# GpSimd's residual sums without the wait for the unpacking of the last weight block

## The chip, the cores and the metric

One core of a Trainium2 chip. The metric is the device time of the program in microseconds; the median of three runs counts. The profile shows one execution, with a span (first to last instruction) a little shorter than its device time.

## The reference

The input x has 64 batches of 64 rows by 1024 columns. Each batch picks one of 16 condition matrices (64 x 64), which mixes its rows; the result goes through a linear layer with a 1024 x 1024 weight, given as packed 6-bit integers with a scale and a zero point for each output column, and is added to x:

```python
def cond(x, weights, condition):
    W = weights[condition]
    return jnp.einsum('bct,bcd->bdt', x, W)

def ffn(x, qweight, weight_scale, weight_zero_point, bias):
    w = dequantize(qweight)   # four 6-bit values from three int32 words
    w = (w - zero_point) * scale
    return jnp.einsum('bsk,nk->bsn', x, w) + bias

x = x + ffn(cond(x, cond_weights, itok), qweight, scale, zero_point, bias)
```

## The kernel before, in words

Two batches make one tile of 128 rows, so there are 32 tiles (counted from 0). Four tiles are in flight in rings of four buffers (`RING`). The work of a tile goes round the engines:

- SyncE's queue loads x (`x_sb`) and two condition matrices (`w_sb`), and stores the two halves of the output.
- TensorE mixes (`mix`, line 264), which also transposes, into PSUM (`y_ps`). ScalarE copies that to `y_hi` (line 415) and VectorE writes the remainder `y_lo` (`low`, line 507). TensorE then multiplies both with the unpacked weight `qT`, one half of the output columns at a time (`linear`, `products`, line 306), into `o_ps`.
- ScalarE sums the rows of x (`sum_x`), TensorE mixes those sums (`sum_y`), and VectorE uses them for the zero point.
- GpSimd writes x plus the bias to `resid` (`add_bias`, line 624). VectorE adds the zero-point term to `resid` (`residual`, line 516), scales the products from PSUM into `o_sb` (`scale_out`, line 527) and adds `resid` to them (`add_residual`, line 535).

The weight comes in eight blocks of 128 output columns (`NT` is 8, blocks 0 to 7). For each, VectorE unpacks the words into 16-bit integers with three instructions (`unpack_q`, lines 495, 497 and 499, each adding 1 to the semaphore `q_part`), TensorE transposes them (`transpose_q`, line 288), and ScalarE places them in `qT` (`place_q`, line 429). These blocks are woven by hand into the work of the first tiles. VectorE's order there is: blocks 0 to 3, low parts of tile 0, the zero-point rows, blocks 4 to 6, low parts of tile 1, scaling of tile 0's first half, block 7, scaling of tile 1's first half, low parts of tile 2, then residuals. TensorE's order is: the first products of tile 0, mix of tile 1, block 4, rest of tile 0's first half, block 5, `sum_y(0)`, block 6, half of tile 1's products (these reuse the bank that the scaling of tile 0 frees), block 7, the other half, mix of tile 2, and so on. After tile 3 loops take over, with two tiles to a step.

On GpSimd the program clears two buffers, builds the identity, waits for the bias (loaded by SyncE's queue after the weight blocks), waits for all of `q_part`, and then adds the bias to tile after tile. Tiles 0 to 3 wait only for their x; from tile 4 on a sum also waits until VectorE has written the output of the tile four before, whose buffer it takes. A reload of an x buffer waits, among other things, for the sum of the tile before in it (`xbias_ready`). Every engine works through its own list in order.

Of the kernel before, what the change touches and what calls it, by code (L numbers as in the profile page):

```python
# [31 lines left out]
def adaln_ffn(nc: bass.Bass, x, cond, weights, qweight, scale, zero, bias, out):  # L32
    B, C, K = x.shape
    NCOND, _, S = weights.shape
    N, KP = qweight.shape
    assert C == S == P // 2 and N == K
    G = KP // 3
    KT = K // P
    NT = N // P
# [13 lines left out]
    with ExitStack() as ctx:  # L53
# [6 lines left out]
        def sem(name):  # L60
            return ctx.enter_context(nc.semaphore(name))
# [54 lines left out]
        q_part = sem("q_part")  # L116
# [18 lines left out]
        def x_arrived(eng, j, i):  # L135

            eng.wait_ge(x_loaded[j % RING], (i + j // RING + 1) * 16)
# [9 lines left out]
        def _(sp):  # L147
# [31 lines left out]
            def store_last():  # L179
                t = TILES - 1  # L180
                store(t % RING, t // RING, 0)
                for n, (_, col, width) in enumerate(last_pieces):
                    sp.wait_ge(o_ready[1], t + 1 + n)
                    sp.dma_start(out_rows[t * P:(t + 1) * P, col:col + width],
                                 o_sb[:, t % 2, col:col + width]).then_inc(o_stored[1][t % 2], 16)
# [423 lines left out]
        @block.gpsimd  # L609
        def _(pool):  # L610
            nc.gpsimd.memset(w_sb[:], 0.0).then_inc(w_zeroed, 1)
            nc.gpsimd.memset(ident[:], 0.0).then_inc(blank_ready, 1)
            pool.wait_ge(blank_ready, 1)
            nc.gpsimd.affine_select(out=ident[:], in_=ident[:], compare_op=ALU.not_equal, fill=1.0, base=0,
                                    pattern=[[-1, P]], channel_multiplier=1).then_inc(ident_ready, 1)
            pool.wait_ge(bias_loaded, 16)
            pool.wait_ge(q_part, 3 * NT)

            def add_bias(j, i):
                x_arrived(pool, j, i)  # L620
                if not isinstance(i, int) or i * RING + j >= RING:
                    for h in range(H):
                        pool.wait_ge(o_ready[h], i * RING + j - RING + 1)
                nc.gpsimd.tensor_tensor(resid[:, j % RING, :], x_sb[:, j % RING, :], bias_bc[:],  # L624
                                        ALU.add).then_inc(xbias_ready, 1)

            for j in range(RING):
                add_bias(j, 0)
            with pool.Fori(1, TRIPS) as i:
                for j in range(RING):  # L630
                    add_bias(j, i)
# [23 lines left out]
```

## Time and profile before

| what | value |
|---|---|
| median of 3 runs | 298.5 us |
| lowest, highest | 298.39, 301.09 us |
| the profiled execution's own time | 301.04 us |
| its span | 299.1 us |
| TensorE busy | 293.5 us (98%) |
| VectorE busy | 185.2 us (62%) |
| GpSimd busy | 90.7 us (30%) |
| ScalarE busy | 78.9 us (26%) |

The page gives the granted clock of TensorE as full in all of its 40 slices. Busy time is the time in which an engine has at least one instruction in work. Matmuls overlap, so TensorE's 98% means that it hardly ever stood idle, not that it worked at its peak. PE is TensorE, DVE is VectorE, ACT is ScalarE, POOL is GpSimd, and SPq is SyncE's queue.

### The profile page before, as it was taken

To read this page: it belongs to the slowest core of one execution; us is meant where nothing else is said; L and a number is where in the kernel's file an instruction comes from. 1 tells how busy PE (TensorE), PEld (TensorE's weight loads), DVE (VectorE), ACT (ScalarE), POOL (GpSimd) and SP (SyncE) were. 2 spreads that over 40 slices of the span, in tenths; PEclk is the share of its full clock that TensorE was granted. 3 is DMA by queue.
4 is the path that set the end of the run, shared out by engine and by line. 5 is a ranking of instruction groups with operands and counts; after the bars stand their busy time and mean duration, and the time that the engine had idled before them with its cause. 6 is when DMAs were issued, how large, how long until landed. Compare 5 with 4: busy or idle time off the path is not lost.

```text
span 299.1 us, 8384 instructions
## 1 busy us (share of the span) xinstructions
PE 293.5 (98%) x3245; PEld 243.5 (81%) x3245; DVE 185.2 (62%) x254; ACT 78.9 (26%) x171; POOL 90.7 (30%) x39
## 2 busy tenths in 40 slices
PE   8999998999999999999999999999999999999995
PEld 3688876888888888888888888888888888888885
DVE  3544896675656656585665667565665658566554
ACT  3438324250503204050402305050320505020000
POOL 1005844234334042434314143433404243430000
PEclk9999999999999999999999999999999999999999
DMA  6950175452442515234342425234241520111211
GB/s 241 328 223 15 65 249 206 168 181 77 147 147 83 172 70 182 105 113 144 139 134 82 153 105 173 82 142 147 84 170 70 184 105 35 70 72 60 82 70 70
DMA packets 20404, 38.49 MB, mean 129 GB/s; under 512 B 6820, under 2 KB 7076, under 8 KB 20390
## 3 DMA queue, kind: packets, MB, share of 16 engines
q1 hardware_dynamic: 20098, 37.50, 36.4%
q10 hardware_dynamic: 292, 0.79, 0.7%
q8 instruction: 10, 0.16, 0.2%
q14 instruction: 4, 0.03, 0.0%
HBM read 21.50 MB, written 16.78 MB: 128 GB/s over the span
## 4 chain that ended last, share of the span: by engine, by line
PE 93%; DVE 4%; issue 2%; ACT 0%; DVEq 0%
PE o_ps L306 75%; PE y_ps L264 11%; PE y_ps L329 2%; PE ysum_ps L278 2%; DVE resid L516 1%; PE qt_ps L288 1%; PE o_ps L288 1%; DVE y_lo L507 1%; PE ysum_ps L326 1%; PE o_ps L329 1%; PE y_ps L306 1%; DVE o_sb L527 1%; DVE o_sb L535 1%; ACT y_hi L415 0%; DVE o_sb L603 0%
## 5 line engine op out<-in xcount | busy, mean ns | idle before, releaser
L306 PE MATMUL o_ps<-qT,y_hi 128*128 128x512 f32 (+1 forms) x520 | 201.2, 391 | 1.1 <-DVE o_sb L527 1.1
L306 PE MATMUL o_ps<-qT,y_lo 128*128 128x512 f32 (+1 forms) x520 | 199.0, 387 | 0.0
L624 POOL TENSOR_TENSOR resid<-x_sb,bias_bc 128x1024 f32<-128x1024 f32 x32 | 89.5, 2802 | 176.6 <-DVE o_sb L535 152.5
L306 PEld LDWEIGHTS o_ps<-qT,y_hi 128*128 128x128 f32 x520 | 98.0, 190 | 20.9 <-DVE o_sb L527 1.2
L306 PEld LDWEIGHTS o_ps<-qT,y_lo 128*128 128x128 f32 x520 | 98.0, 190 | 18.8
L527 DVE TENSOR_TENSOR o_sb<-o_ps,scale_bc 128x512 f32<-128x512 f32 x63 | 43.6, 692 | 85.0 <-PE o_ps L306 84.9
L415 ACT ACTIVATE y_hi<-y_ps 128x512 fp32r<-128x512 f32 x64 | 33.4, 602 | 175.3 <-PE y_ps L264 175.3
L535 DVE TENSOR_TENSOR o_sb<-o_sb,resid 128x512 f32<-128x512 f32 x63 | 51.7, 820 | 2.3
L507 DVE TENSOR_TENSOR y_lo<-y_ps,y_hi 128x512 fp32r<-128x512 f32 x64 | 40.0, 684 | 13.1 <-ACT y_hi L415 13.1
L516 DVE SCALAR_TENSOR_TENSOR resid<-zs_bc,ysum,resid 128x1024 f32<-128x1024 f32 x32 | 41.9, 1310 | 0.0
L264 PE MATMUL y_ps<-w_sb,x_sb 64*64 64x64 f32 x2048 | 35.1, 223 | 0.0
L406 ACT ACTIVATE junk<-x_sb 128x1024 bf16<-128x1024 f32 x32 | 34.1, 1089 | 0.0
L264 PEld LDWEIGHTS y_ps<-w_sb,x_sb 64*64 64x64 f32 x2048 | 32.5, 138 | 1.7 <-issue 1.5
L278 PEld LDWEIGHTS ysum_ps<-xsum,w_sb 128*128 128x128 f32 x64 | 9.7, 189 | 1.4
L278 PE MATMUL ysum_ps<-xsum,w_sb 128*128 128x1 f32 x64 | 8.5, 230 | 0.0
L495 DVE TENSOR_SCALAR q_int<-q_raw 128x256 int16<-128x256 int16 x8 | 3.6, 455 | 6.6 <-DMA q_raw<-in_L_ffn_qweight_dram 6.6
L406 ACT ACTIVATION_READ_ACCUMULATOR junk<-x_sb 128x1 f32 x32 | 7.4, 231 | 0.0
L424 ACT ACTIVATE ysum<-ysum_ps 128x1 f32<-128x1 f32 x32 | 4.5, 202 | 3.9 <-PE ysum_ps L278 3.9
L429 ACT ACTIVATE qT<-o_ps 128x1024 fp32r<-128x1024 int16 x4 | 4.1, 1028 | 4.0 <-PE o_ps L288 4.0
L288 PEld LDWEIGHTS o_ps<-ident,q_int 128*128 128x128 bf16 x32 | 2.4, 118 | 3.3 <-issue 1.8
L429 ACT ACTIVATE qT<-qt_ps 128x1024 fp32r<-128x1024 int16 x4 | 4.1, 1030 | 0.4 <-PE qt_ps L288 0.4
L497 DVE TENSOR_SCALAR q_int<-q_raw 128x256 int16<-128x256 int16 x8 | 4.0, 501 | 0.0
(32 smaller groups left out, 40.2 us busy)
## 6 DMA issues: line engine op xcount, KB each, us to landing
x_sb<-in_x_dram SPq DMA_DIRECT2D x32, 512.0 KB, 3.5
out_dram<-o_sb SPq DMA_DIRECT2D x63, 256.0 KB, 2.0
q_raw<-in_L_ffn_qweight_dram SPq DMA_DIRECT2D x6, 384.0 KB, 4.9
w_sb<-in_L_cond_weights_dram SPq DMA_DIRECT2D x64, 16.0 KB, 2.0
q_raw<-in_L_ffn_qweight_dram ACTq DMA_DIRECT2D x2, 384.0 KB, 5.4
bias_bc<-in_L_ffn_bias_dram SPq DMA_DIRECT2D x1, 512.0 KB, 7.4
out_dram<-o_sb SPq DMA_DIRECT2D x2, 128.0 KB, 1.9
ids<-in_itok_B_dram SPq DMA_DIRECT2D x1, 0.2 KB
```

What stands on the lines that cost most here:

```text
L264: last = nc.tensor.matmul(y_ps[part * Q:(part + 1) * Q, j % 2, half, kt, :], x_sb[rows, slot, k0:k0 + Q], w_sb[rows, slot, rows], start=Tr ...
L278: nc.tensor.matmul(ysum_ps[:, slot:slot + 1], w_sb[:, slot, :], xsum[:, slot:slot + 1], start=True, stop=True).then_inc(ysum_ps_ready, 1)
L288: last = nc.tensor.transpose(qt_banks[n % 2][:, kt, :], q_cols[:, n % 4, kt * P:(kt + 1) * P], ident[:])
L306: last = nc.tensor.matmul(bank, part[:, slot, kt, :], qT[:, kt, col:col + width], start=(kt == 0 and part is y_hi), stop=(kt == KT - 1 and ...
L329: nc.tensor.matmul(bank, ones[:], row[:, h * NH:(h + 1) * NH], start=True, stop=True).then_inc(row_ps_ready, 1)
L406: nc.scalar.activation(junk[:, j % 2, :], x_sb[:, j % RING, :], ACT.Copy, accum_out=xsum[:, j % RING:j % RING + 1]).then_inc(xsum_ready, 1)
L415: nc.scalar.activation(y_hi[:, j % RING, :, cols], y_ps[:, j % 2, half, :, :], ACT.Copy).then_inc(y_hi_ready, 1)
L507: nc.vector.tensor_tensor(y_lo[:, j % RING, :, cols], y_ps[:, j % 2, half, :, :], y_hi[:, j % RING, :, cols].bitcast(F32), ALU.subtract).t ...
L516: nc.vector.scalar_tensor_tensor(resid[:, j % RING, :], zs_bc[:], ysum[:, j % RING:j % RING + 1], resid[:, j % RING, :], ALU.mult, ALU.add ...
L527: nc.vector.tensor_tensor(o_sb[:, j % 2, cols], o_ps[:, h, :], scale_bc[:, cols], ALU.mult).then_inc(scaled[h], 1)
L535: nc.vector.tensor_tensor(o_sb[:, j % 2, cols], o_sb[:, j % 2, cols], resid[:, j % RING, cols], ALU.add).then_inc(o_ready[h], 1)
L624: nc.gpsimd.tensor_tensor(resid[:, j % RING, :], x_sb[:, j % RING, :], bias_bc[:], ALU.add).then_inc(xbias_ready, 1)
```

## The change

GpSimd no longer waits until all 24 unpacking instructions (three for each of the eight blocks) are done before its first sum. The wait for the bias and each sum's wait for its x stay.

```diff
             pool.wait_ge(bias_loaded, 16)
-            pool.wait_ge(q_part, 3 * NT)
 
             def add_bias(j, i):
                 x_arrived(pool, j, i)
```

## Rows read from the trace of the kernel before

**Rows 1.** The page: span, and busy us by engine.

```profile
span 299.1 us, 8384 instructions
PE 293.5 (98%) x3245; PEld 243.5 (81%) x3245; DVE 185.2 (62%) x254; ACT 78.9 (26%) x171; POOL 90.7 (30%) x39
```

**Rows 2.** Waits, whole span: engine, line, waited for, us, times, longest.

```profile
POOL resid L624 <- DVE q_int L499: 24.1, 1, 24.1
...
PE o_ps L306 <- DVE o_sb L527: 1.1, 1, 1.1
```

**Rows 3.** Timeline of DVE, 31 to 46 us: start, duration, operation.

```profile
31.46 1.29 DVE L507 TENSOR_TENSOR y_lo<-y_ps,y_hi 128x512 fp32r<-128x512 f32 x2 [1.16 <-ACT y_hi L415]
32.66 1.52 DVE L516 SCALAR_TENSOR_TENSOR resid<-zs_bc,ysum,resid 128x1024 f32<-128x1024 f32 x1
34.28 2.70 DVE L535 TENSOR_TENSOR o_sb<-o_sb,resid 128x512 f32<-128x512 f32 x1
36.91 1.27 DVE L516 SCALAR_TENSOR_TENSOR resid<-zs_bc,ysum,resid 128x1024 f32<-128x1024 f32 x1
38.29 0.69 DVE L535 TENSOR_TENSOR o_sb<-o_sb,resid 128x512 f32<-128x512 f32 x1
...
45.44 0.67 DVE L527 TENSOR_TENSOR o_sb<-o_ps,scale_bc 128x512 f32<-128x512 f32 x1
```

**Rows 4.** Timeline of POOL, 26 to 37 us: the first and fourth sum.

```profile
26.00 2.39 POOL L624 TENSOR_TENSOR resid<-x_sb,bias_bc 128x1024 f32<-128x1024 f32 x1 [24.09 <-DVE q_int L499]
...
33.06 3.38 POOL L624 TENSOR_TENSOR resid<-x_sb,bias_bc 128x1024 f32<-128x1024 f32 x1
```

**Rows 5.** The bias: its issue in the timeline, and its landing by tile.

```profile
10.85 0.44 SPq L199 DMA_DIRECT2D bias_bc<-in_L_ffn_bias_dram  x1
...
DMA to landing us min/median/max: 7.4/7.4/7.4
```

**Rows 6.** Timeline of PE, 25 to 46 us.

```profile
25.12 0.48 PE L306 MATMUL o_ps<-qT,y_hi 128*128 128x512 f32 x1
...
27.05 0.62 PE L288 MATMUL o_ps<-ident,q_int 128*128 128x128 bf16 x8
...
43.61 1.16 PE L264 MATMUL y_ps<-w_sb,x_sb 64*64 64x64 f32 x64
...
46.16 0.50 PE L306 MATMUL o_ps<-qT,y_hi 128*128 128x512 f32 x1 [1.08 <-DVE o_sb L527]
```

**Rows 7.** Timeline of DVE, 18 to 26 us: end of block 5, block 6, block 7.

```profile
18.08 0.47 DVE L499 TENSOR_SCALAR q_int<-q_raw 128x512 int16<-128x512 int16 x1
18.47 0.46 DVE L495 TENSOR_SCALAR q_int<-q_raw 128x256 int16<-128x256 int16 x1
18.70 0.51 DVE L497 TENSOR_SCALAR q_int<-q_raw 128x256 int16<-128x256 int16 x1
18.99 0.47 DVE L499 TENSOR_SCALAR q_int<-q_raw 128x512 int16<-128x512 int16 x1
22.39 1.29 DVE L507 TENSOR_TENSOR y_lo<-y_ps,y_hi 128x512 fp32r<-128x512 f32 x2 [2.93 <-ACT y_hi L415]
24.24 0.69 DVE L527 TENSOR_TENSOR o_sb<-o_ps,scale_bc 128x512 f32<-128x512 f32 x1 [0.57 <-PE o_ps L306]
24.85 0.45 DVE L495 TENSOR_SCALAR q_int<-q_raw 128x256 int16<-128x256 int16 x1
...
25.38 0.48 DVE L499 TENSOR_SCALAR q_int<-q_raw 128x512 int16<-128x512 int16 x1
```

**Rows 8.** The chain of work that ended last, by time: start, us, what.

```profile
16.97 3.52 PE o_ps L306 x16
...
22.25 1.96 PE o_ps L306 x16
```

## The prediction

> **What bounds the kernel now.** I read the busy line first: TensorE is busy for 293.5 of 299.1 us, so a change is worth only what it adds to or takes from TensorE's idle time or the length of its work [rows 1]. Then the waits: GpSimd's sums sat behind the unpacking of the last weight block for 24.1 us, the wait that the change removes, and nothing in TensorE's list names GpSimd. TensorE's one large wait behind another engine's work in the steady run is 1.1 us, for VectorE's scaling of an output tile [rows 2]. Last the timelines of the four engines between 18 and 46 us. The reader is to see there that GpSimd and VectorE hold each other up, and which of these waits reach TensorE.
>
> How they hold each other up: VectorE's first residual addition (line 535) took 2.70 us at 34.28, where the same form takes 0.69 us [rows 3]. It therefore began at 34.28 + 2.70 - 0.69 = 36.29 us, while GpSimd's fourth sum ended at 33.06 + 3.38 = 36.44 us [rows 4]. That sum was itself about 1.0 us longer than the 2.39 us of the first: VectorE's line 516, issued at 32.66 and finished at 34.18, had gone ahead of it [rows 3, 4]. So for operations of VectorE with two inputs in SBUF, one of the two waits until the other has quite finished. Line 507, with one input in PSUM, took 1.29 us for two at 31.46, in the middle of the third sum, and wasn't held up [rows 3]: it still costs 0.64 us apiece.
>
> **What the change removes.** The sums may start once the bias has landed: its DMA is issued at 10.85 and lands 7.4 us later, at 18.25 us [rows 5]. Tile 0 and 1 of x were requested before it on the same queue. GpSimd began 0.14 us after what it waited for (25.86 to 26.00), so the four sums move from 26.0 to 36.4 us to about 18.4 to 28 us: 7.6 us earlier [rows 4, 7]. No instruction is added or dropped.
>
> **The gain.** TensorE waits 1.08 us before 46.16 for the scaling of tile 1's second half, which VectorE starts at 45.44 and finishes 0.67 us later [rows 3, 6]. VectorE was busy without a gap worth naming from 31.46 to there, and inside this stretch it lost 1.52 - 1.27 = 0.25 us to the third sum and 2.70 - 0.69 = 2.01 us to the fourth [rows 3]. With the sums over by 29 us, both go: 2.26 us. The scaling could then begin at 43.2, but the products that it reads end only where TensorE's next mix starts, at 43.61 [rows 6]. So it begins at about 43.7 and ends at about 44.4, before TensorE asks for it at 46.16 - 1.08 = 45.08. The whole 1.08 us goes, and no more: what is late next is TensorE's own work. GpSimd's fifth sum, triggered by VectorE's output of tile 0, moves along with VectorE and keeps its place relative to it. The x tiles of the second round are requested earlier, since that request waits for the first sum, and this hides behind work that TensorE has until then; it is worth nothing.
>
> **The cost.** Two unpackings now lie beside the sums: block 6 (18.47 to 19.46) and block 7 (24.85 to 25.86) [rows 7]. Each is three instructions of one input in SBUF, and no row of this trace shows such a one beside a sum; that is the disputed price. Below: nothing, if they don't meet. Above: a whole sum for each meeting, 2.3 us or so. I take it that they meet, because of their pace: starts 0.39 us apart for 512 columns (18.08 to 18.47) and 0.23 for 256 (18.47 to 18.70) make 0.16 / 256 = 0.6 ns a column, against (1270 - 690) / 512 = 1.1 ns for lines 516 and 535 [rows 3, 7]. They move about two elements where the others move one, so something more of the port is used.
>
> The Trainium skill says the same from the other side (VectorE: DVE Perf Modes, Mode 2x_2P; SBUF — State Buffer, Who interferes with whom): a one-source operation from SBUF to SBUF with an even outermost count takes both port pairs, one of which is GpSimd's, and the one that starts first blocks the other fully. By that rule this change puts a lock in front of the unpacking, and it speaks against the change; the pace and the 2.70 us above agree with it, the unpacking beside a sum is not shown.
>
> What is queued behind a held unpacking: VectorE works in order. Behind block 6 stand the low parts of tile 1 (22.39, two of 0.65 us) and the scaling of tile 0 (24.24 to 24.93), whose bank TensorE takes for tile 1 at 25.12: 0.2 us of cover [rows 6, 7]. Behind block 7 stands TensorE itself, which transposes it at 27.05: 1.2 us of cover after 25.86 [rows 6, 7].
>
> Now in turns. At the end of the third sum the waiting line 516 was served ahead of the fourth [rows 3, 4]. I assume the same both ways: whoever waits goes next, also between two unpacking instructions. A sum holds VectorE off for about 2.3 us (2.39 less the 0.15 us between 36.29 and 36.44), an instruction of the unpacking holds off the sum for 0.25 to 0.4 us. GpSimd is ready at 18.4, in the middle of the row of unpackings; three places of entry:
> (a) Before block 6's first instruction: sum 0 to 20.7, first instruction to 20.95, sum 1 to 23.2, second to 23.5, sum 2 to 25.8, third to 26.2; the low parts to 27.5, the scaling to 28.1, block 7 after sum 3 (28.5) to 29.5. TensorE starts tile 1 at 28.2 in place of 25.12: 3.1 us late; block 7 is in time for it.
> (b) After the first: third instruction done at 24.0, low parts 25.2, scaling 25.8; block 7's first at 26.5, sum 3 to 28.8, its last at 29.5. TensorE transposes at 29.55 in place of 27.05: 2.5 us late.
> (c) After the second: block 6 done at 21.7, nothing of it felt; block 7 as in (b): 2.45 us late.
> I take 2.5 us. Less the gain of 1.08, this is +1.4 us (+2.0 for (a)).
>
> **The sum.** The profiled execution took 301.04 us for a span of 299.1; the median of the runs is 298.5 and the highest 301.09, so the profiled one is at the slow edge. I add the difference to the median: 298.5 + 1.4 = 299.9 us. A median of a few runs of this kernel can be told from no change at about 1%, 3 us, so nearly every case here lies within that.
>
> **The rivals.**
> - Unpacking in one piece: VectorE, once served, keeps the port for its three pipelined instructions (their starts are closer than their durations of 0.46 us [rows 7], which speaks for it). Block 7 then starts at 26.3 and is done 1.0 us later at 27.3: 0.2 us late. 0.2 - 1.1 = -0.9: 297.6 us.
> - No meeting at all, so the change doesn't have the cost that I see: -1.1, 297.4 us. Against it stands the pace of the unpacking.
> - GpSimd holds on (slower): its four sums are queued without a wait between them, and if it keeps the port through all four, VectorE is held from 18.4 to about 27.8. Block 6 is done at 28.8, low parts 30.1, scaling 30.8: TensorE takes tile 1 5.7 us late; +4.6, 303.1 us. It makes the kernel slower by over 1% from the point at which TensorE is held there for over 4.1 us. Against it: line 516 got in ahead of the fourth sum [rows 3, 4].
> - TensorE's pace falls: at 16.97 sixteen products of 256 columns took 3.52 us, and the same sixteen at 22.25 took 1.96 us, a ratio of 1.8, near that of 2.4 to 1.2 GHz, while the page shows the granted clock full throughout [rows 8]. If an idle stretch of 2.5 to 3 us near 27 brings back a slow stretch as long as that one, it adds 3.52 - 1.96 = 1.6 us: +3.0, 301.5 us. Against it: the idle 1.08 us before 46.16 changed nothing, though it is shorter.
>
> **How the numbers follow.** Turns 0.44 (299.9, 299.5 to 300.5 by the place of entry), one piece 0.26, no meeting 0.12, GpSimd holds on 0.08, slow pace 0.06, something unseen 0.04. The range reaches from the two gaining cases with a little spread, 297.1, to the slow pace, 301.6, and leaves out GpSimd holding on and the unseen. Faster by over 1% would need 3 us where only 1.1 us of idle time is there: 0.03. Slower by over 1%: GpSimd holding on, half of the slow pace, and a share of the unseen: 0.13. Within 1%: 0.84.
>
> **What the profile of the changed kernel would show.** GpSimd's first sum at 18.3 to 18.5; if later, my landing time is off. Unpacking instructions of block 6 or 7 that last about 2.5 us in place of 0.46, one between every two sums (turns), one at the head of a block alone (one piece), or none (no meeting). TensorE's idle stretch before the transposes at 27.05 or before tile 1's products at 25.12: 2 to 3 us, or 0.2. No wait of TensorE before linear products at 46, and line 535's first at 0.69 us. The pace of products after the idle stretch: starts 0.23 us apart or twice that. The forecast is wrong if GpSimd is not let in between unpackings, or if TensorE's wait at 46 stays, for instance because the fifth sum now meets VectorE in a worse place.

## The result, and the profile after

The changed kernel took 303.05 us (median of 4 runs, 302.66 to 303.94) against 298.44 us before: a ratio of 1.0133 (95% interval 1.0068 to 1.0199). By the two medians it is 4.6 us slower, by the ratio 4.0 us, and the interval lies wholly above 1; forecast was 299.9 us, range 297.1 to 301.6. The two profiled executions are nearer to each other: 301.04 us (span 299.1) before, 303.94 us (span 302.0) after.

The page of the changed kernel, its span and busy line:

```profile
span 302.0 us, 8384 instructions
PE 295.0 (98%) x3245; PEld 244.5 (81%) x3245; DVE 189.7 (63%) x254; ACT 79.0 (26%) x171; POOL 90.1 (30%) x39
```

TensorE's large waits, but for one of 1.2 us in the warm-up that both kernels have:

```profile
PE o_ps L306 <- DVE o_sb L527: 1.3, 1, 1.3
PE qt_ps L288 <- DVE q_int L499: 1.2, 1, 1.2
```

Against [rows 2], the one wait of 1.1 us late in the weaving is gone, and two others have come, both earlier, both behind VectorE: for block 6 of the weight, and for the scaling of tile 0. (The line `o_ps L306 <- DVE o_sb L527` looks as before, but it is another wait, at 27.89.)

VectorE's timeline, the answer to [rows 7] and the first part of [rows 3]:

```profile
18.08 0.47 DVE L499 TENSOR_SCALAR q_int<-q_raw 128x512 int16<-128x512 int16 x1
18.47 2.63 DVE L495 TENSOR_SCALAR q_int<-q_raw 128x256 int16<-128x256 int16 x1
20.90 2.66 DVE L497 TENSOR_SCALAR q_int<-q_raw 128x256 int16<-128x256 int16 x1
23.35 2.59 DVE L499 TENSOR_SCALAR q_int<-q_raw 128x512 int16<-128x512 int16 x1
25.86 1.27 DVE L507 TENSOR_TENSOR y_lo<-y_ps,y_hi 128x512 fp32r<-128x512 f32 x2
27.06 0.68 DVE L527 TENSOR_TENSOR o_sb<-o_ps,scale_bc 128x512 f32<-128x512 f32 x1
27.66 0.83 DVE L495 TENSOR_SCALAR q_int<-q_raw 128x256 int16<-128x256 int16 x1
...
38.14 0.69 DVE L535 TENSOR_TENSOR o_sb<-o_sb,resid 128x512 f32<-128x512 f32 x1
```

The three instructions of block 6 last 2.63, 2.66 and 2.59 us where they lasted 0.46, 0.51 and 0.47. The two low parts at 25.86 and the scaling at 27.06 are not longer at all, though GpSimd is still adding: each has one of its two inputs in PSUM. They are only late. And the first residual addition, 2.70 us before, takes 0.69 us.

GpSimd's four sums in the same time:

```profile
18.23 2.54 POOL L623 TENSOR_TENSOR resid<-x_sb,bias_bc 128x1024 f32<-128x1024 f32 x1 [16.32 <-DMA bias_bc<-in_L_ffn_bias_dram]
20.73 2.50 POOL L623 TENSOR_TENSOR resid<-x_sb,bias_bc 128x1024 f32<-128x1024 f32 x1
23.19 2.47 POOL L623 TENSOR_TENSOR resid<-x_sb,bias_bc 128x1024 f32<-128x1024 f32 x1
25.62 2.54 POOL L623 TENSOR_TENSOR resid<-x_sb,bias_bc 128x1024 f32<-128x1024 f32 x1
```

The first starts with the landing of the bias. Each of the three instructions of block 6 was held through one sum and ended as the next began: 18.47 + 2.63 = 21.10, 20.90 + 2.66 = 23.56, 23.35 + 2.59 = 25.94, each about 0.35 us after the start of the next sum. So it is one instruction of the one engine, then one of the other.

TensorE, to be laid beside [rows 6]:

```profile
26.00 0.62 PE L288 MATMUL qt_ps<-ident,q_int 128*128 128x128 bf16 x8 [1.23 <-DVE q_int L499]
27.89 0.77 PE L306 MATMUL o_ps<-qT,y_hi 128*128 128x512 f32 x1 [1.26 <-DVE o_sb L527]
28.45 0.63 PE L306 MATMUL o_ps<-qT,y_lo 128*128 128x512 f32 x1
28.88 0.63 PE L306 MATMUL o_ps<-qT,y_hi 128*128 128x512 f32 x1
...
31.15 0.62 PE L288 MATMUL o_ps<-ident,q_int 128*128 128x128 bf16 x8
...
49.08 0.48 PE L306 MATMUL o_ps<-qT,y_hi 128*128 128x512 f32 x1
```

The products of tile 1 start at 27.89 in place of 25.12, 2.77 us late. They then start 0.43 us apart (28.45 to 28.88) where the fast pace is 0.23, so that block 7's transposes are at 31.15 in place of 27.05: 4.10 us late. The products at 49.08, before at 46.16, are 2.92 us late: 1.18 us have come back. From there to the end both executions take the same time (302.0 - 49.08 and 299.1 - 46.16, both 252.9 us), so the whole loss lies ahead of it. The windows show the granted clock (the figure ahead of the last two) over this stretch:

```profile
28.00:32.00 4.00, 4.00 (x18) 3.11 (x19) 1.03 (x3) 0.91 (x3) 0.16 (x1) 0.65 0.06 12
32.00:36.00 4.00, 4.00 (x79) 3.42 (x78) 1.13 (x2) 2.08 (x4) 0.00 (x0) 1.00 0.01 4
```

In 28 to 32 us it is 0.65 of full on average, so most of the stretch ran at the level of 1.2 GHz and the rest at 2.4. Just before, TensorE had been idle for 1.23 us (up to 26.00) and for 1.26 us (up to 27.89).

### The profile page after: what moved, and what is told of

Same layout as the page of the kernel before. It is cut to its first block, busy times and chain, and to the rows that moved or that the text cites. A ratio compares the mean times of both kernels' runs of the same rounds, so it can differ in the third digit from the quotient of the medians.

```text
span 302.0 us, 8384 instructions
## 1 busy us (share of the span) xinstructions
PE 295.0 (98%) x3245; PEld 244.5 (81%) x3245; DVE 189.7 (63%) x254; ACT 79.0 (26%) x171; POOL 90.1 (30%) x39
## 4 chain that ended last, share of the span: by engine, by line
PE 95%; DVE 4%; issue 1%; DVEq 0%
PE o_ps L306 77%; PE y_ps L264 11%; PE y_ps L329 2%; PE ysum_ps L278 2%; DVE q_int L495 1%; DVE q_int L497 1%; PE ysum_ps L326 1%; PE o_ps L329 1%; PE qt_ps L288 1%; PE y_ps L306 1%; PE o_ps L288 0%; DVE y_lo L507 0%; DVE q_int L499 0%; DVE o_sb L527 0%; DVE o_sb L603 0%
## 5 line engine op out<-in xcount | busy, mean ns | idle before, releaser
L306 PE MATMUL o_ps<-qT,y_hi 128*128 128x512 f32 (+1 forms) x520 | 202.1, 392 | 1.3 <-DVE o_sb L527 1.3
L306 PE MATMUL o_ps<-qT,y_lo 128*128 128x512 f32 (+1 forms) x520 | 199.7, 388 | 0.0
L306 PEld LDWEIGHTS o_ps<-qT,y_hi 128*128 128x128 f32 x520 | 98.5, 191 | 21.3 <-DVE y_lo L507 1.4
L306 PEld LDWEIGHTS o_ps<-qT,y_lo 128*128 128x128 f32 x520 | 98.6, 191 | 19.0
L527 DVE TENSOR_TENSOR o_sb<-o_ps,scale_bc 128x512 f32<-128x512 f32 x63 | 43.6, 691 | 86.0 <-PE o_ps L306 85.8
L535 DVE TENSOR_TENSOR o_sb<-o_sb,resid 128x512 f32<-128x512 f32 x63 | 49.6, 788 | 2.3
L495 DVE TENSOR_SCALAR q_int<-q_raw 128x256 int16<-128x256 int16 x8 | 6.2, 775 | 6.4 <-DMA q_raw<-in_L_ffn_qweight_dram 6.4
L497 DVE TENSOR_SCALAR q_int<-q_raw 128x256 int16<-128x256 int16 x8 | 6.1, 767 | 0.0
L429 ACT ACTIVATE qT<-o_ps 128x1024 fp32r<-128x1024 int16 x4 | 4.1, 1024 | 7.1 <-PE o_ps L288 7.1
L499 DVE TENSOR_SCALAR q_int<-q_raw 128x512 int16<-128x512 int16 x8 | 5.8, 727 | 0.0
```

The lines of the kernel that those rows point to most:

```text
L306: last = nc.tensor.matmul(bank, part[:, slot, kt, :], qT[:, kt, col:col + width], start=(kt == 0 and part is y_hi), stop=(kt == KT - 1 and ...
L495: nc.vector.tensor_scalar(to[:, :, 0], words[:, :, 0, 0], QMASK, None, ALU.bitwise_and).then_inc(q_part, 1)
L497: nc.vector.tensor_scalar(to[:, :, 1], words[:, :, 0, 0], QBITS, QMASK, ALU.logical_shift_right, ALU.bitwise_and).then_inc(q_part, 1)
L527: nc.vector.tensor_tensor(o_sb[:, j % 2, cols], o_ps[:, h, :], scale_bc[:, cols], ALU.mult).then_inc(scaled[h], 1)
L535: nc.vector.tensor_tensor(o_sb[:, j % 2, cols], o_sb[:, j % 2, cols], resid[:, j % RING, cols], ALU.add).then_inc(o_ready[h], 1)
```

## The experiments

Ratios are against the kernel before, run beside each on the same chip. The kernel before has three groups of times: of 85 executions 23 took 297.2 to 297.6 us, 26 took 298.1 to 298.8, and 36 took 300.75 us or more (all but one under 301.6). A median of a few runs can fall into any of them.

**The kernel before again, and the change again.** No edit.

> The kernel before, unchanged, to learn how far its executions differ. Theory (turns at the port, and TensorE's slower pace after an idle stretch of 2.5 us): a ratio of 1.00, median 298.4 us, and no unpacking instruction over 0.6 us. What is open: the profiled execution of before took 301.0 us against 298.4 of the median. If its early stretch at the slow pace (16.97, 3.52 us for 16 products) is what differs, a faster profiled execution shows that stretch shorter. Rival (the loss of the change is drift between executions): ratio off 1 by as much as the change's 1.013.

Measured: 299.64 us, ratio 1.0014 (0.997 to 1.0058). So the change's 4.0 us and more are not drift. This profiled execution took 297.51 us, span 295.6, and is of the lowest group. The chain of work that ended last (start, us, what):

```profile
15.08 1.97 PE o_ps L306 x16
18.69 1.96 PE o_ps L306 x16
```

The first sixteen products of 256 columns take 1.97 us here, at 15.08, and took 3.52 us at 16.97 in the profile before [rows 8]. The next sixteen take 1.96 us in both, only 3.56 us earlier here, and the executions are 3.53 us apart. So what separates the lowest group from the highest, as far as one profile of each shows, is when TensorE's early slow pace ends, at 20.4 us or before 14.5, before the sums even begin. The middle group of the kernel before has no profile. The Trainium skill says (TensorE: Matmul & The Clock Gate, Part 1, The HAM clock gate) that the watch on its activity runs freely and doesn't start with the kernel; a spread of this kind agrees with that.

> The changed kernel again, in more rounds. Theory: TensorE starts tile 1's products 2.8 us late, has a slow stretch that costs 1.4 us more, and gets 1.1 us back at 46: +3.1 us, ratio 1.010, and up to 1.015 where before happens to run without a slow stretch of its own. Rival (drift between executions): a ratio of 1.00 within 0.003.

Measured: 303.0 us (301.84 to 305.35), ratio 1.0105 (1.0057 to 1.0153). The loss is there again, 3.1 us by the ratio and 4.4 by the medians. The profiled execution, 305.35 us, is the longest of all: block 6 was held as before (2.64, 2.66 and 2.59 us), but the slow stretch lasted longer, with a granted clock of 0.50 in 28 to 32 us and still 0.53 in 32 to 34. No execution of the changed kernel is in the two lower groups: its lowest of all is 301.84 us.

**The change a third time.** No edit.

> The changed kernel once more, for a profile of an execution whose early slow stretch ends early, if it is one. Theory: then block 6 is done before the first sum and isn't held, and block 7 is held at each of its three instructions; a slow stretch follows where TensorE was idle for over 2.5 us. Rival (VectorE is held at the same place in every execution): block 6 is held as in the two profiles so far.

Measured: 303.45 us, span 301.5. It was again an execution with a long early slow stretch, so that it doesn't test what happens after a short one. But here the bias landed later, the first sum started at 18.77 in place of 18.23, and VectorE's timeline shows another place of entry:

```profile
18.47 0.46 DVE L495 TENSOR_SCALAR q_int<-q_raw 128x256 int16<-128x256 int16 x1
...
18.99 2.58 DVE L499 TENSOR_SCALAR q_int<-q_raw 128x512 int16<-128x512 int16 x1
...
24.74 1.75 DVE L495 TENSOR_SCALAR q_int<-q_raw 128x256 int16<-128x256 int16 x1
26.29 2.61 DVE L497 TENSOR_SCALAR q_int<-q_raw 128x256 int16<-128x256 int16 x1
```

Two instructions of block 6 are through before the sum gets in, and only the third is held. The low parts are then in time, and it is block 7 that is late: held by 1.3 and by 2.1 us, and TensorE waits 2.1 us for it. A slow stretch followed here too, from about 30.6, though the idle time was less than the 2.5 us of the expectation. Half a microsecond of the bias decides where VectorE is caught, and TensorE loses its two to three microseconds either way.

**The sums wait for block 6 only.**

```diff
             pool.wait_ge(bias_loaded, 16)
+            pool.wait_ge(q_part, 3 * (NT - 1))
```

> The sums wait for block 6 but not for block 7. Theory of turns: block 6's three instructions are at 0.46 us again, block 7's first instruction waits from 24.85 to about 26.6, the fourth sum goes between the first and the second, the block is done at about 29.5; TensorE transposes it at 29.6 in place of 27.05 (2.5 us late); less 1.1 us at 46: +1.4 us, or +2.9 with a slow stretch after the idle time (299.9 to 301.3). Rival (VectorE keeps the port for its three pipelined instructions): block 7 done at 27.6, +0.5 - 1.1 = -0.6 us (297.8). Rival (the loss came through something else than the port, say the earlier x loads): as slow as the change, 303.

Measured: 303.53 us, ratio 1.0131 (1.0083 to 1.0178): no better than without any wait. VectorE's timeline, and TensorE's wait for block 7:

```profile
22.18 1.34 DVE L495 TENSOR_SCALAR q_int<-q_raw 128x256 int16<-128x256 int16 x1
23.32 2.63 DVE L497 TENSOR_SCALAR q_int<-q_raw 128x256 int16<-128x256 int16 x1
25.75 2.56 DVE L499 TENSOR_SCALAR q_int<-q_raw 128x512 int16<-128x512 int16 x1
```

```profile
PE o_ps L288 <- DVE q_int L499: 3.8, 1, 3.8
```

This execution had another start than both profiles of before: the pace was fast from about 12, the granted clock fell at 15.0, with TensorE at work, and was full again at 18.4. So block 7 came at 22.2 and not at 24.85, under the second sum and not under the third, and was held three times. The mechanism is the one expected, turn by turn, its size 1.3 us larger; a slow stretch followed. The forecast of +1.4 to +2.9 us was too low, and the rival of one piece is out. The other rival, that the loss comes from something else such as the earlier x loads, had forecast 303 us, and the time alone fits it; the 3.8 us that TensorE waits for held unpackings speak against it, and so does the next run.

Block 6 was done at 17.41 here, and the first sum waited for the bias, until 18.45. The added wait had no effect, so this is also what the changed kernel does after such a start. The profiled execution took 302.73 us. The profiles of two_in_gap, halves, only_writes and filled have the same start and no other slow stretch on record, and their granted clock over the whole execution is 0.993 or 0.994; the executions of before at 0.992 to 0.994 are its middle group, 298.1 to 298.8 us. If they start alike, the change costs about 4.3 us there.

**Two sums in the gap.** As above, and the third sum waits for block 7:

```diff
             for j in range(RING):
+                if j == 2:
+                    pool.wait_ge(q_part, 3 * NT)
                 add_bias(j, 0)
```

> The sums of tiles 0 and 1 wait for block 6 only and fall into the gap between blocks 6 and 7 (19.5 to 24.85 us, two sums of 2.4), the sums of tiles 2 and 3 wait for block 7 as before. Theory: no unpacking instruction is held, the first residual addition takes 0.69 us in place of 2.70, TensorE's wait of 1.08 us before 46.16 is gone: -1.1 us, 297.3, ratio 0.996. Rival (early sums cost by themselves, through the x loads that they release): slower than before. If the second sum ends after 24.85, block 7 is late by the difference, which its cover of 1.2 us hides.

Measured: 297.6 us, ratio 0.9967 (0.9927 to 1.0006), so by the interval it is not told from no change. Set side by side by clock it stands out: eight of the twelve executions took 297.0 to 297.9 (most of them 297.0 to 297.4) at a granted clock of 0.992 to 0.994, where those of before at that clock took 298.3 to 298.8. If a like clock means a like early stretch, that is about 1.1 us less, the wait that the prediction counted on. VectorE's timeline:

```profile
22.06 0.99 DVE L495 TENSOR_SCALAR q_int<-q_raw 128x256 int16<-128x256 int16 x1
22.84 0.50 DVE L497 TENSOR_SCALAR q_int<-q_raw 128x256 int16<-128x256 int16 x1
...
31.25 0.69 DVE L535 TENSOR_TENSOR o_sb<-o_sb,resid 128x512 f32<-128x512 f32 x1
```

Block 7's first instruction meets the end of the second sum and is held 0.5 us, which its cover hides, and the first residual addition takes 0.69 us. TensorE has no wait behind VectorE left after the warm-up. Two early sums with their early x loads cost nothing that can be measured here, which speaks against the rival of the early loads (those released by the sums of tiles 2 and 3 stay late in this run).

**Sums cut into pieces.** For tiles 0 to 3, `PIECES` instructions on a share of the columns, with a second semaphore (`xpart`) that keeps the waits of VectorE and SyncE's queue complete. The main part of the edit:

```diff
-                nc.gpsimd.tensor_tensor(resid[:, j % RING, :], x_sb[:, j % RING, :], bias_bc[:],
-                                        ALU.add).then_inc(xbias_ready, 1)
+                pieces = PIECES if first else 1
+                for n in range(pieces):
+                    cols = slice(n * K // pieces, (n + 1) * K // pieces)
+                    nc.gpsimd.tensor_tensor(resid[:, j % RING, cols], x_sb[:, j % RING, cols], bias_bc[:, cols],
+                                            ALU.add).then_inc(xbias_ready if n == pieces - 1 else xpart, 1)
```

> The changed kernel, with the sums of tiles 0 to 3 cut into two instructions of 512 columns each. Theory of turns, instruction by instruction: an unpacking instruction waits for one half sum (about 1.25 us) and not 2.4, so block 6's three last about 1.4 us each and the block is done near 22.4, before the low parts need VectorE; block 7's three are spread over about 3.8 us from 24.85 and TensorE gets it 1.6 us late: +0.6 us against before, or +2 with a slow stretch. Rival (the port time of a tile's sum counts as a whole, however it is cut): block 6 as late as in the change, 25.9, and a ratio of 1.010 to 1.013.

Measured: 301.05 us, ratio 1.0044 (0.9994 to 1.0094). Block 7 on VectorE:

```profile
22.21 1.46 DVE L499 TENSOR_SCALAR q_int<-q_raw 128x256 int16<-128x256 int16 x1
23.46 1.56 DVE L501 TENSOR_SCALAR q_int<-q_raw 128x256 int16<-128x256 int16 x1
24.82 1.49 DVE L503 TENSOR_SCALAR q_int<-q_raw 128x512 int16<-128x512 int16 x1
```

> The changed kernel, with the sums of tiles 0 to 3 cut into four instructions of 256 columns each. Theory of turns: an unpacking instruction waits for one quarter (about 0.7 us); block 6 is done near 21, block 7 near 27.1, which its cover of 1.2 us hides but for 0.1; the wait of 1.08 us at 46 is gone: -0.9 us, ratio 0.997. Rival (the port time counts as a whole): 1.010 to 1.013.

Measured: 300.01 us, ratio 1.002 (0.9974 to 1.0065). Block 7 on VectorE:

```profile
21.25 0.50 DVE L499 TENSOR_SCALAR q_int<-q_raw 128x256 int16<-128x256 int16 x1
21.55 1.00 DVE L501 TENSOR_SCALAR q_int<-q_raw 128x256 int16<-128x256 int16 x1
22.35 0.97 DVE L503 TENSOR_SCALAR q_int<-q_raw 128x512 int16<-128x512 int16 x1
```

The time that an instruction is held follows the size of the one that holds it: 2.6 us long beside a sum of 1024 columns, 1.5 beside 512, 1.0 beside 256. That is the turn, instruction by instruction. TensorE waits 1.8 us for block 7 with halves and not at all with quarters. The medians are moved about by the groups; the three shortest executions with quarters took 296.4 us, against 297.3 in the lowest group of before (0.9 less, as expected), and the shortest with halves 298.1 (0.8 more, one execution). No slow stretch followed the 1.8 us of idle time with halves.

**TensorE kept busy in the wait.** `fill(5)` issues five products of blank data into a bank that is free there. Its calls:

```diff
             sum_y(0, 0)
+            fill(5)
             transpose_q(6)
+            fill(5)
             wait_linear(1, 0, 0)
```

> The changed kernel, with ten products of blank data (about 0.22 us each) on TensorE in its idle stretch: five before the transposes of block 6, five before tile 1's products. Theory (the idle stretch of 2.5 us brings the slow pace back): the products of tile 1 start 0.23 us apart at once, the granted clock stays full between 28 and 32, and 1.4 to 2.9 us of the change's loss go; tile 1 starts as late as in the change. About 301 us, ratio 1.007 against before. Rival (the slow stretch has nothing to do with the idle time): the slow stretch stays and the time is as in the change, 303.

Measured: 302.3 us, ratio 1.0125 (1.0067 to 1.0182). TensorE's timeline where it waits for block 7, and the window that was slow in the change:

```profile
27.83 0.62 PE L288 MATMUL o_ps<-ident,q_int 128*128 128x128 bf16 x8 [1.36 <-DVE q_int L506]
28.26 0.47 PE L306 MATMUL o_ps<-qT,y_hi 128*128 128x512 f32 x1
28.57 0.39 PE L306 MATMUL o_ps<-qT,y_lo 128*128 128x512 f32 x1
```

```profile
28.00:32.00 4.00, 4.00 (x84) 3.53 (x82) 0.69 (x1) 1.59 (x3) 0.00 (x0) 1.00 0.00 0
```

The products after the wait start at the fast pace and the granted clock is full, against 0.65 in the change. But this is not the test that was planned. The execution started like that of wait_block6, block 6 was not held, and the fills ran at 22.07 and 23.37, where TensorE had work waiting; they put off tile 1's products by some 2 us. The idle time before block 7 stood behind them and was not filled, only shortened to 1.36 us from the 3.8 us of wait_block6. What the profiles show together is an order: a slow stretch followed idle times of 1.23 and 1.26 us close together, 1.34 and 1.26, 2.10, and 3.83, and none followed single ones of 0.86, 1.36 and 1.80. That the idle time brings the slow pace back agrees with this and is not proved by it, the less so as the clock of wait_block6 also fell at 15.0 without an idle TensorE. The gain, 0.7 us of the median where about 2 were expected, is smaller because the fills cost time themselves; the 302.3 us are not explained to the microsecond.

**Only writes.** The sums of tiles 0 to 3 become two clearings each; x and bias are left out of those tiles, which makes its output another one. The main part of the edit:

```diff
+                if isinstance(i, int) and i * RING + j < RING:
+                    nc.gpsimd.memset(resid[:, j % RING, :], 0.0).then_inc(xset, 1)
+                    pool.wait_ge(xset, j + 1)
+                    nc.gpsimd.memset(resid[:, j % RING, :], 0.0).then_inc(xbias_ready, 1)
+                    return
```

> The changed kernel, with the sums of tiles 0 to 3 replaced by two clearing instructions each, which read nothing (so x and bias are left out of tiles 0 to 3). Theory (an unpacking instruction in its two-port mode needs the port's write side too): each unpacking instruction that meets a clearing one waits for it, and lasts well over 0.5 us. Rival (only the read side is shared): all unpacking instructions take 0.46 to 0.51 us.

Measured: one execution, 297.13 us. VectorE's block 7, and GpSimd's clearing at that time:

```profile
22.17 1.03 DVE L496 TENSOR_SCALAR q_int<-q_raw 128x256 int16<-128x256 int16 x1
23.00 0.50 DVE L498 TENSOR_SCALAR q_int<-q_raw 128x256 int16<-128x256 int16 x1
23.29 0.45 DVE L500 TENSOR_SCALAR q_int<-q_raw 128x512 int16<-128x512 int16 x1
```

```profile
22.83 1.82 POOL L625 MEMSET resid<- 128x1024 f32 x1
```

The first unpacking instruction is held to 1.03 us by a clearing, which reads nothing, and the next clearing waits in turn: 1.82 us where the others take 0.95. So the unpacking is held by a GpSimd that only writes. The Trainium skill says (SBUF — State Buffer, Who interferes with whom) that an operation in a two-port mode contends with GpSimd for the whole shared pair, a reading and a writing port, and sets an operation with two inputs in SBUF apart, which should mind only a GpSimd that reads. The trace agrees with the first half, by the 1.03 us; the second was not tried. The turns are not one by one here: the clearing issued at 22.83 ended at 24.65, so its 0.95 us began at about 23.70, and all three unpackings had gone ahead of it. Strict turns are shown where whole or cut sums follow one another and unpackings meet them; they are no rule for every case.

**More warm-up, before and after.** `WARMUP` 12 in place of 5, on the kernel before, the change, and the two sums in the gap.

> The kernel before with 12 warm-up products on TensorE in place of 5. The executions of before fall into three groups, 297.3, 298.5 and 301.1 us, and the two profiled ones differ in when TensorE's slow pace ends (before 15 or at 20.4 us). Theory (that early slow stretch makes the groups): with TensorE busy without a gap from 1.2 to 6.3 us the slow stretch ends early in every execution, the products at 16 are at the fast pace, and all executions lie within 0.5 us of each other near 297.3 to 298. Rival (the groups have another origin): three groups 3.8 us wide as before, all of them later by what the seven products delay.

Measured: 297.59 us (295.37 to 300.92), ratio 0.9934 (0.9892 to 0.9976). The single group that I expected did not come. The windows of the profiled execution (300.92 us) show why:

```profile
10.00:16.00 6.00, 6.00 (x69) 3.18 (x60) 2.98 (x6) 2.79 (x4) 0.00 (x0) 0.50 0.95 315
16.00:20.00 4.00, 4.00 (x24) 3.95 (x24) 3.44 (x10) 2.06 (x3) 0.00 (x0) 0.50 0.98 354
```

Eight transposes that began at 7.51 took 0.62 us and eight at 11.38 took 1.03: the pace had risen, and fell again from 10 to 20 us. In this execution the better start didn't hold through the small pieces of work there. It was the highest of the twelve; ten took at most 298.75, which is why the median gains.

> The changed kernel with 12 warm-up products. Theory: TensorE's needs come earlier, as in the fast executions, so block 6 is unpacked before the sums start and block 7 meets them: TensorE waits for it some 3 us or more, gets 1.1 us back, and in most executions has a slow stretch after it: +3 to +6 us against warm_before, and the spread of the group before is gone, so the difference shows clearly. Rival (the loss comes only in executions with a long early slow stretch): the same time as warm_before.

Measured: 302.45 us, ratio 1.0126 (1.0067 to 1.0185); 4.9 us above the median of the warm kernel before. Six executions took 301.55 to 304.62 us, and one 297.29, which is the profiled one. VectorE and GpSimd in it:

```profile
21.29 0.45 DVE L495 TENSOR_SCALAR q_int<-q_raw 128x256 int16<-128x256 int16 x1
21.53 0.52 DVE L497 TENSOR_SCALAR q_int<-q_raw 128x256 int16<-128x256 int16 x1
21.82 2.63 DVE L499 TENSOR_SCALAR q_int<-q_raw 128x512 int16<-128x512 int16 x1
```

```profile
21.30 2.86 POOL L623 TENSOR_TENSOR resid<-x_sb,bias_bc 128x1024 f32<-128x1024 f32 x1
```

Here the sum came 10 ns after block 7's first instruction, and two instructions were through before it was let in (it lasted 2.86 us, 0.5 of it waiting). Only the third is held, TensorE waits 0.9 us, and the freed 1.1 us pays for that. It is the same mechanism at its cheapest.

> Two sums in the gap between blocks 6 and 7, with 12 warm-up products. Theory: block 7 comes earlier than in the slow executions (at about 21 to 22 us), so it meets the second sum, is held once and for at most 1.5 us, which its cover mostly hides; the wait of 1.08 us is gone: 0.5 to 1.1 us faster than warm_before. Rival (early sums cost by themselves): not faster than warm_before.

Measured: 297.42 us, ratio 0.9949 (0.9907 to 0.999) against before, but 0.2 us from the warm kernel before with the usual sums. What was expected, 0.5 to 1.1 us, is not shown.

## Why the prediction was wrong

The mechanism of the main case was right. The sums started at 18.23 (forecast 18.3 to 18.5). They and the unpacking took turns, instruction by instruction, at place (a). Place (a) was reckoned at 3.1 us late for tile 1's products; it was 2.77. Block 7 was in time, as said for (a). The wait at 46 went away, 1.08 us reckoned and 1.18 found. What failed is the sum: it left out one term, took another from the cheaper place, and was added to the wrong base.

- **"TensorE's pace falls", 0.06, as a rival to the turns.** This step failed first: the slow pace was left out of the main sum. It isn't a rival to the turns; it comes on top of them. It came after the idle time in all three profiles of the change and in that of wait_block6. In the profiled execution the chain gives 3.42 us for eight products of 512 columns where before these took 1.90, which is 1.5 us; I had 1.6 us, with the wrong chance. From start to start up to block 7's transposes it is 4.10 - 2.77 = 1.33 us, and with that the way from 46.16 to 49.08 is 2.77 + 1.33 - 1.18 = 2.92 us, and the profiled executions are 2.90 us apart. That it follows from the idle time is argued from the order of idle times above, and no run tested it alone.
- **"I take 2.5 us", places (b) and (c).** The place depends on the landing of the bias within half a microsecond: (a) in two profiles, (c) in the third, where the delay was 2.1 us at block 7 (reckoned 2.45). I took the cheaper place; against the 2.77 us measured at (a) that is 0.3 us too little.
- **"I add the difference to the median."** By the medians it is worth 4.6 - 2.9 = 1.7 us. I knew that the profiled execution was at the slow edge and did not ask what separates the executions. It was in the row that I had in hand, [rows 8]: the early slow stretch. The median of before, 298.4, lies in the middle group; the timeline on which I reckoned belongs to the group of 301 us. 301.04 + 2.90 = 303.94, while the median moved by 4.6 us. In executions whose slow stretch ends earlier, VectorE has block 7 at 21 to 22 us, under the second sum, and can be held at all three of its instructions, which cost 3.8 us in wait_block6: 302.73 us, some 4.3 more than the middle group. The changed kernel itself was not profiled in such an execution; that it loses more there is read from wait_block6, where the added wait had no effect, and from its own eleven executions, none of which is below 301.84 us. Part of the 1.7 us is also luck of a median of four: over all executions the mean is 303.2 us for the change and 299.3 before, 3.9 us.

The other rivals: beside the sums one piece is out (three of three instructions were held apart), no meeting is out, and GpSimd did not hold on through its four sums. Its forecast, 303.1 us, is nearly what was measured, and yet nothing of it took place: the time alone would have confirmed the wrong story.

The range was too narrow at the top because the slow pace stood beside the turns and not on top of them: 299.9 + 1.6 is 301.5, and place (a) with it 302.1. Even that is about 1 us short of the measured median.

## What to carry to other kernels

Beside an engine that shares a port, price each short instruction at the whole length of the other's, and count how many of them stand in a row: three instructions of about 0.5 us took 6.4 us more of VectorE's time here. Freed early work belongs in a gap that is long enough for it, or in pieces so small that what they hold up stays within the cover (with quarters 1.0 us in all at block 7, under a cover of 1.2). Before a difference is added to a median, find out what separates the executions, and place the timeline in the group to which it belongs.

## What the runs showed that I had not expected

- The kernel before has three groups of times, 3.8 us from the lowest to the highest, and the profiles tie them to TensorE's pace before 20.4 us: slow throughout in the highest, fast from before 14.5 in the lowest, and, if its granted clock is a sign of it, fast and then slow once more from about 15 to 18 in the middle one. In the profile of the highest group the granted clock reads 1.00 during the slow stretch, though the same sixteen products take 3.52 us and not 1.97: only the pace shows it.
- An unpacking instruction of 512 columns and one of 256 are held alike (2.59 and 2.63 us); what counts is the sum beside it: 2.6, 1.5 and 1.0 us for 1024, 512 and 256 columns.
- A clearing instruction, which reads nothing, holds an unpacking (0.46 us became 1.03) and is held by three of them in a row (0.95 us became 1.82).
